# Second layer's attention: the values matmuls between the second turn and the middle scores, and VectorE's emptying of bank P one step later

## The reference

```python
xn = _layernorm(x, axis=-1)
q, k, v = ...            # xn @ qkv, 16 heads of 64
s = q @ k.T / sqrt(64) + bias[h, i - j]      # j <= i only
out = softmax(s) @ v @ out_w
x = x + out + moe_ffn(xn)
```

## Time and profile before

| | |
|---|---|
| median of three runs | 2357.43 us (2355.05 to 2363.06) |
| span of the profiled execution | 2391.1 us |
| PE busy | 2121.2 us, 89% |
| DVE, ACT, POOL busy | 1636.0, 1318.1, 941.8 us |
| granted TensorE clock, mean | 0.943 |

### The profile page before, as it was taken

How to read it: one execution, slowest core, us unless ns; L and a number is a source line. 1 busy time by engine, 2 the same in 40 slices (tenths; PEclk the granted TensorE clock), 3 DMA queues, 4 the chain that set the end, 5 groups by cost and what they waited for, 6 DMA issues and landing times. The chain is left out here.

```text
span 2391.1 us, 51165 instructions
## 1 busy us (share of the span) xinstructions
PE 2121.2 (89%) x19252; PEld 1329.9 (56%) x19252; DVE 1636.0 (68%) x4801; ACT 1318.1 (55%) x2688; POOL 941.8 (39%) x1175
## 2 busy tenths in 40 slices
PE   4679998998999999999999697799999985899876
PEld 2447776996667776777777565233333333333333
DVE  7665653675555566666666554799899955588896
ACT  2246765555666677777777433167666673323312
POOL 2036665663557743565433122111111110054462
PEclk8689999999999999999999899599999998999998
DMA  6311112214011100000000035211111101000000
GB/s 174 115 52 34 36 33 63 74 37 144 17 35 17 34 6 7 15 2 19 2 2 2 11 97 164 59 36 37 37 39 45 43 7 37 0 0 0 9 9 18
DMA packets 77908, 93.78 MB, mean 39 GB/s; under 512 B 10145, under 2 KB 56242, under 8 KB 76002
## 3 DMA queue, kind: packets, MB, share of 16 engines
q1 hardware_dynamic: 64178, 77.23, 10.8%
q0 software_dynamic: 13488, 13.28, 2.8%
HBM read 54.55 MB, written 35.53 MB: 38 GB/s over the span
## 5 line engine op out<-in xcount | busy, mean ns | idle before, releaser
L1069 ACT ACTIVATE WA<-a_E 128x1024 f32<-128x1024 f32 (+1 forms) x320 | 282.9, 939 | 126.5 <-PE a_E L1002 68.1
L982 PE MATMUL a_S<-a_KS,a_QS 54*128 54x512 bf16 (+3 forms) x768 | 201.8, 352 | 38.2 <-DVE a_mx L1104 27.1
L455 POOL TENSOR_SCALAR WA<-WA,a1b_rinv 128x1024 f32<-128x1024 f32 (+3 forms) x192 | 140.5, 747 | 236.6 <-DVE a1b_rinv L754 236.5
L747 DVE COPY a1b_PT<-a1b_A 128x512 f32<-128x512 f32 x96 | 66.3, 691 | 183.4 <-PE a1b_A L554 183.4
L572 PE MATMUL a1b_O<-a1b_PT,WA 128*64 128x128 f32 x3072 | 190.0, 277 | 0.8 <-DVE WA L747 0.8
L572 PEld LDWEIGHTS a1b_O<-a1b_PT,WA 128*64 128x64 f32 x3072 | 167.0, 137 | 41.2 <-issue 34.3
L535 PE MATMUL a1b_B<-a1b_Kf,a1b_Qf 64*128 64x512 f32 (+2 forms) x768 | 187.2, 484 | 1.3 <-DVE a1b_firstmax L741 1.1
L455 POOL TENSOR_SCALAR XR<-XR,a1b_rinv 128x768 f32<-128x768 f32 (+3 forms) x192 | 140.8, 748 | 115.9 <-DVE a1b_rinv L754 115.9
L982 PEld LDWEIGHTS a_S<-a_KS,a_QS 54*128 54x128 bf16 x768 | 53.5, 94 | 205.1 <-DVE a_mx L1104 97.1
L1020 PE MATMUL a_O<-WA,V 128*9 128x512 f32 (+3 forms) x1536 | 158.0, 499 | 0.1
L1102 DVE TENSOR_REDUCE a_mx<-a_S 128x1 f32<-128x512 f32 x256 | 156.8, 681 | 1.7 <-PE a_S L982 1.7
(11 more groups left out here) (497 smaller groups left out, 5382.5 us busy)
## 6 DMA issues: line engine op xcount, KB each, us to landing
WA<-in_w SPq DMA_DIRECT2D x8, 1024.0 KB, 9.2
a_QS<-qstack SPq DMA_DIRECT2D x32, 216.0 KB
a_KS<-kstack SPq DMA_DIRECT2D x32, 216.0 KB
a1b_tb<-tab SPq DMA_DIRECT2D x12, 512.0 KB
qstack<-f_parts SPq DMA_DIRECT2D x24, 256.0 KB
kstack<-f_parts SPq DMA_DIRECT2D x24, 256.0 KB
f_slots<-f1r_zrows SPq DMA_DIRECT2D x9, 516.0 KB
f1t_xs<-f_slots SPq DMA_DIRECT2D x9, 516.0 KB, 7.1
```

The source lines that it names most:

```text
L455: pool.tensor_scalar(v, v, rinv[:, e, u, part:part + 1], 1.0, ALU.mult, ALU.mult).then_inc(n_sb, 1)
L982: ins = pe.matmul(pS[(at + half) % SB][:, lo:lo + n], QS[s][ROW[half], pair, i * P:(i + 1) * P], KS[s][ROW[half], pair, c * CH:c * CH + n] ...
L1069: act.activation(PT[q % NP][:, :, 0:w], pE[q % 2][:, :, 0:w], ACT.Exp).then_inc(e_sb, 1)
```

## The change

TensorE issues `values(step - 1)` after turn 1 and not at the end of the step. ScalarE takes the exponential of head 1's first part before it copies turn 2 and not after. VectorE takes the reciprocal of head 0 before the middle minima; it copies the queries out of bank P one step later (e = 1), and adds bank P into x one step later (e = 0 of the next iteration), both behind the wide minima. The count that the join waits for follows the new order, and one addition more stands behind the loop. All operations stay, none is added.

```diff
@@ TensorE
                     turn(step, 1)
+                    if step:
+                        values(step - 1)
                     scores(step + 2, 1)
                     scores(step + 2, 2)
                     turn(step, 2)
@@
                         project(pC[1], it + 2, 0, 0)
-                    if step:
-                        values(step - 1)
             values(ALL - 1)
@@ ScalarE
                     exponential(step + 1, 1, 0)
+                    exponential(step + 1, 0, 1)
                     copy(step, 2)
-                    exponential(step + 1, 0, 1)
                     exponential(step + 1, 1, 1)
@@ VectorE
                     for u in range(HG):
                         bias(step + 2, order[0], u)
+                    if e == 0:
+                        add(pP, it - 2, 1, 2 * step)
+                    if e == 1:
+                        project_q(pP, it + 1, 1)
+                    inverse(step + 1, 0)
                     bias(step + 2, order[1], 0)
                     copy(step, 2)
                     bias(step + 2, order[1], 1)
-                    inverse(step + 1, 0)
                     for u in range(HG):
                         bias(step + 2, order[2], u)
                     inverse(step + 1, 1)
-                    if e == 0:
-                        project_q(pP, it + 1, 1)
                     if e == 2:
                         add(pC[1], it - 1, 0, 2 * step)
                     if e == 3:
-                        add(pP, it - 1, 1, 2 * step)
                         project_q(pC[1], it + 2, 0)
                     if join:
                         for hook in (2 * step, 2 * step + 1):
-                            join["vector"](dve, hook, x_sb, max(0, 2 * (it - 1) + max(0, e - 1)))
+                            join["vector"](dve, hook, x_sb, max(0, 2 * (it - 1) + (e > 1)))
+            add(pP, IT - 2, 1, 2 * ALL)
             add(pC[1], IT - 1, 0, 2 * ALL)
             add(pP, IT - 1, 1, 2 * ALL)
```

## The result

The changed kernel takes 2347.19 us (median of four runs, 2346.08 to 2347.68). The kernel before, timed beside it, takes 2358.89 us (2355.05 to 2363.06). The ratio is 0.9946, 95% interval 0.9933 to 0.996: a gain of 11.7 us, where 41.3 was forecast. The time lies outside the range of 2293 to 2336.

A forecast was written before the change was run, and what follows sets the result against it. TensorE was taken as full, losing time to waits for emptied banks; afterwards a 7.61 us chain decides. Gains 9.5 + 25.1 + 10.6 + 1.9 - 5.2 = 41.9, scaled to 41.3, gave 2316 us, range 2293 to 2336.

The forecast's parts named there:

- the base: Whole kernel: timed median 2357.43 taken as 0.986 of the profiled span, so a gain of 41.9 us becomes 41.3.
- These two terms: Second layer's attention: 26 steps gain 9.5 us and 32 gather steps 25.1 us, at 7.61 us a step.
- The long step: One 12.4 us step between the ordinary steps of the second part: taken as 10.5 after the change, a gain of 1.9.
- The chain: Turn 1, values, middle scores, minima, reciprocal of head 1, GpSimd's scaling, next turn 1: about 7.61 us a step.
- TensorE's work: TensorE in an ordinary step: 7.80 less 0.33 of waiting, plus 0.09 at a join, a floor of 7.56 us.
- Rival B: TensorE's work decides at 7.47 us a step because the chain is shorter: 16 us better, 2300 us; chance 0.20.
- The swap on ScalarE: Exponential of head 1's first part before turn 2's copy: costs nothing; old order would end the last exponential near 7.4.
- Head 0's reciprocal: On VectorE ahead of the middle minima: GpSimd starts head 0 at 4.1, not 6.5; otherwise the chain is 0.7 longer.
- Bank P: VectorE's two emptyings, 0.6 us each, behind the next wide minima: nothing waits; at the old place they would wait.
- The last three steps: End of each part, without projections to hide the chain: from 20.6 and 19.8 to 22.8 us, a loss of 5.2.
- Rival C: Gather and scatter steps: lateness of 0.6 falls into the chain, 58 steps take 8.2, 2351 us; chance 0.10.
- Rival D: VectorE and GpSimd exclude each other, 0.75 per step in the chain, steps 8.36, 2406 us; chance 0.05.

The follow-up runs named there:

- e1: The kernel before, unchanged, profiled a second time: 2359.42 us against 2359.89 for the kernel before beside it (0.9999).
- e4: The changed kernel with VectorE's reciprocal of head 1 moved ahead of the two narrow minima: 2326.90 us, 0.9854 of the kernel before.
- e6: The changed kernel with the reciprocal of head 0 back behind the middle minima: 2452.58 us, 1.0391 of the kernel before.
- e3: The kernel before with only ScalarE's and VectorE's edits, values left at the end of the step: 2399.91 us, 1.0169 of the kernel before.
- e7: The changed kernel with both emptyings of bank P at their old place: 2346.67 us, 0.9942 of the kernel before.
- e15: The kernel before, unchanged, profiled on the chip of e8: 2406.69 us.
- e9: e4 with the values ahead of turn 1 and three exponentials on ScalarE before the copy of turn 1: 2378.47 us, 0.9889 of the kernel before.
- e18: The kernel before with GpSimd's indirect DMAs waiting for ScalarE's copy of turn 0, on a fifth chip: 2396.08 us against 2393.54 (1.0012).
- e8: The kernel before, unchanged, a third profile, on another chip: 2404.54 us.
- e12: The changed kernel, unchanged, on the chip of e8: 2347.14 us, 0.9762 of the kernel before.

## Why the prediction was wrong

**The failed step is the base.** "The median of the shown runs, 2357.43, is 0.986 of this span; 41.9 becomes 41.3". A factor of 0.986 says that all stretches of the timed runs are a little shorter, and changes the sum by 0.6 us only. In fact 57 ordinary steps had the same length to 0.1%, and 26.4 of the 30.1 us between the first profile and e1 lay in the scatter and gather steps, from which I took 34.6 of the 41.9 us. These two terms, 9.5 and 25.1, are 2.4 and 3.7 from e1 to the kernel after (201.36 - 198.94 and 248.33 - 244.60). The kernel before takes 2359 to 2362 us in the first pair and on three chips of the experiments, 2393.5 on one and 2406 on one; the first profile, with 2391.1, looks like the slower ones (it has the late copies), the timed runs like the faster. The record doesn't say on which chip either was taken, so this rests on their likeness. The changed kernel takes 2347 on both kinds. So the sum came out near for the profiled execution, 2391.1 - 41.9 = 2349.2 against 2345.2, in part by luck: the ordinary steps gave 7.6 and not 10.6, the long step 2.1 more than forecast, and 5.6 of the 45.9 us lay outside these stretches. It was applied to runs in which the largest term had already vanished. With the stretches of e1 the same sum is 201.4 - 197.9 = 3.5, 248.3 - 243.5 = 4.8, 10.5 for the ordinary steps, 1.9, less 5.2: 15.5, so 2343. The measured 2347.19 is 4 us above that; the spans of e1 and of the kernel after are 15.8 apart, with 13.0 in these stretches. (One sum of the chances was wrong too: "faster" adds up to 0.85, not 0.87.)

**The chain** was right: predicted 7.61, measured 7.64 to 7.66, with the new wait of turn 1 for GpSimd of about 0.1 that was named as its sign. e4 shows that it decides. Single terms were off by up to 0.11 either way (3.51 for 3.41 up to the narrow scores, 0.76 for 0.87 to the copy of turn 2), so the mean is closer than its parts, and one kind of step (e = 0) doesn't wait at all.

**TensorE's work** was 7.56 in the sum and is 7.48 to 7.55. Turn 1 with the values behind it holds 0.59 in e4, the 0.09 of the sum, and middle scores behind the values 0.05 more; turn 2 gives back 0.07, and the narrow scores hold 0.43 where the sum had 0.49. Rival B's case, work alone, isn't what the change reaches, but what e4 does.

**The swap on ScalarE** was named as costing nothing, with the old order setting the chain at 7.4. The last exponential ends at 7.8 and the reciprocal stands at 7.9: the mechanism was right, the size too small.

**Head 0's reciprocal**: 0.7 predicted, 0.83 measured (e6). The half that was not costed is what this place does without the values' move (e3): VectorE waits for ScalarE, in order, with everything behind it.

**Bank P**: "If they stood at the old place they would wait for the P output, which now ends with the step." e7 says no; the projection into C is the last, and the P output is ready before VectorE arrives.

**The long step** fell from 12.4 to 8.39, 4.0 instead of 1.9, and its clock from the earlier trace rows of 0.86 is 1.00: TensorE no longer stands still in it (its narrow scores held 2.85 us in e1, waiting, and hold 0.97). In e1 TensorE was busy 0.36 us from 902 to 904, and from 906 to 908 it was busy throughout at a granted clock of 0.50, the lower of its two levels (1.2 and not 2.4 GHz). The mean of 0.86 over 12.44 us stands for about 3.5 us at that level; by my estimate that is up to 1.7 us, which the forecast didn't count. **The last three steps** did become longer, by 2.4 in each call (22.16 for 19.77 in e1) and not 2.6; but the step behind them gave 2.3 back in the second call (8.96 to 6.67): turn 1 held TensorE for 2.70 us there in e1, waiting, and holds 0.64 now, with the values behind it. I had charged the loss without following its end.

**Rival C** had the nearest time (2351) for another reason. It said that the gather steps' lateness would fall into the chain at 8.2 a step. They take 7.64. **Rival D** is out. GpSimd's scaling keeps 1.47, and VectorE's adds of the joined output, which the earlier trace rows bounded, are not longer than before:

```profile
L1608 DVE TENSOR_TENSOR X<-X,f1acc x16: 404/428/779, 933.0 to 1108.1; 128x256 f32<-128x256 f32 x16
```

The median is 428 ns against 426, the longest 779 against 1177, all 16 together 7.6 us against 9.6. So the 12 us that the prediction allowed for these adds didn't come. The exclusion itself is in the traces. Before, six of the adds start with 0.45 us or more of a scaling of probabilities still to run on GpSimd; they take 726 to 1177 ns and end 0.27 us after that scaling, while the others take 421 to 427. After, four start with 0.25 us or more still to run, take 517 to 779 and end 0.27 to 0.28 after it. Beside eight others, before and after, it is GpSimd's instruction of the join that takes 0.71 to 0.73 us instead of 0.44. The Trainium skill (SBUF — State Buffer, "SBUF: two separate sides") says that a VectorE instruction with two SBUF inputs and a GpSimd instruction that reads SBUF keep each other out, whole instructions at a time. By these adds the trace agrees, and the change made the meetings cheaper.

**What stays open.** Why copies that wait for TensorE start late beside GpSimd's indirect DMA, and on some chips only. Two orders and two turns show that it goes with the DMA, and the two steady distances, about 0.6 and about 1.3 us, tie it to the DMA's start. A DMA that starts 0.55 after the turn (e15) or 0.78 after it (e9, same chip) leaves the copies at 0.76. Whether issue or transfer does it wasn't separated.

## What to carry to other kernels

Before a sum is scaled from a profile to timed runs, ask in which stretch the two differ: here the largest term of the gain was the very excess that the timed runs lacked. When work is moved to cover a wait, move every small instruction that stands ahead of the new chain with it; the reciprocals' and one exponential's places were worth 37 to 105 us, the move itself nothing without them. And once a chain decides a step, look for the instruction in it that could stand earlier: moving one instruction gave another 20 us.

## What the runs showed of the hardware

- On two of five chips the copies of a turn start late when GpSimd starts an indirect DMA in the first 0.0 to 0.5 us of the turn: 1.4 us after the turn instead of 0.76 in most gather steps, 0.9 to 1.05 in most scatter steps (e15; on the second chip e18, for turn 1). On these chips the kernel before takes 33 and 46 us more than its 2360. In the changed kernel, where the DMAs come under turn 1, the late copies cost nothing measurable (2347.14 for 2347.19).
- The late copies start about 0.6 or about 1.3 us after the DMA's start, with issues of 1.01 and of 1.59 us alike (e8, e12, e15, e18).
- An add of two SBUF tensors on VectorE that starts with 0.25 us or more of GpSimd's scaling of probabilities still to run takes 517 to 1177 ns instead of 404 to 436, and ends 0.27 to 0.28 us after that scaling (profiles of before and after).
- Value matmuls behind 64-row transposes: turn 1 holds 0.59 instead of 0.50 us, and the four transposes of turn 2 hold 0.22 instead of 0.27 to 0.29.
- The granted clock was 0.86 in a step of 12.4 us in which TensorE stood still for several us (0.50, the lower level, in the 2 us from 906 in e1), and 1.00 in the same step once it took 8.4.
